# Local attention with the value product one step later, exponentials ahead of the transposed copy, and the row maxima of the cross stage sent from GpSimd's queue

## The chip, the cores and the metric

The kernel runs on one core of a Trainium2 chip. The core has five engines with a queue of instructions each: TensorE (PE in the profile; its weight loads are PEld), VectorE (DVE), ScalarE (ACT), GpSimd (POOL) and SyncE (SP, which here only starts transfers). The queues run side by side and meet only at semaphores. The metric is the device time of one call in microseconds (us), lower is better, taken as the median of three runs.

## What is computed

A batch of 16 rows of 256 tokens and 128 features goes first through one gated cross attention (16 heads of 8) over 1601 context tokens, then through six layers of local attention (16 heads of 64, window 32 and the window before it) and a gated feed-forward.

```python
x = x + jnp.tanh(g_xattn[0]) * xattn(layernorm(x), ctx, ctx, mask, ...)   # softmax over 1601 keys, 16 heads of 8
x = x + jnp.tanh(g_ffn[0]) * ffn(layernorm(x), ...)
# ffn: six times
    x = attn_layer(shift_tokens(x), Wqkv[i], q_scale[i], k_scale[i], Wo[i]) + x
    x = ffn_layer(shift_tokens(x), ln_g[i], ln_b[i], W1[i], b1[i], W2[i], b2[i]) + x
# attn_layer: q and k are brought to length 1, scaled and rotated; then, in each window of 32 queries,
    sim = jnp.einsum('bhwie,bhwje->bhwij', bq, bk2) * QK_SCALE     # keys of this window and the one before
    attn = jax.nn.softmax(jnp.where(mask, -max, sim), -1)
    out = jnp.einsum('bhwij,bhwje->bhwie', attn, bv2)              # then @ Wo
```

## The kernel before

The program has two stages, one behind the other. Nothing is scheduled by a compiler: each engine's queue is written out by hand, and every hand-over is a semaphore wait.

**Cross stage** (`cross_phase`, the first third of the span). It walks over the 16 rows. A row is four quarters `q` of four heads each, and a quarter is 13 key tiles `kt`. For each tile TensorE forms scores in `b_e` (mask L746, then product L750) in two halves, ScalarE exponentiates them to `eT` (L431), and TensorE multiplies them with the values (L652). Beside it the maxima of the next quarter are found (`b_s` L732, VectorE L506) and turned into 4 x 256 numbers `mneg`. `max_parts` (L348 on) splits these on GpSimd into three bf16 parts `mp` with five small operations; three transfers of 2 KB put the parts into rows of the operand `q_op`. Before, the transfers are issued by ScalarE, at tile 9 of each quarter (L475); TensorE waits for them (`mrow_in`) at tile 0 of the next quarter. In the first quarter of a row GpSimd also takes the rest of the key split, `kf` (L368), ahead of `max_parts`, and the last key part `kp` behind it (L384).

**Local stage** (`ffn_phase`, the other two thirds). It walks over 6 x 16 layer-rows. An iteration works on four rows at once, in different states: A makes q, k and v (`b_qk`, L1441 and L1452), B has its scores and probabilities made, C finishes them and goes through the output projection and the first feed-forward product, D ends with the second one (`b_nv`, L1472). It has eight steps `k`, and in each a unit `u` (two pairs of heads for half the queries) passes these stations: `scores(k)` on TensorE into `b_sc` (L1359, L1368); the row maximum and its scaling on VectorE (L1267, then `nb` L1276); four exponentials with sums on ScalarE to `probs` (L1143); reciprocal on VectorE (L1212) and normalising on GpSimd (L1067) a step later; `transposes(u)` on TensorE into `b_pt` (L1380), the copy to `probsT` on ScalarE (L1130) and `values(u)` on TensorE into `b_o` (L1400), all two steps later. VectorE takes `b_o` to `oT` (L1204) in the even steps. `b_sc`, `b_pt` and `b_o` exist once; `scores(k)` waits for `exp_ready`, the exponentials of step k-1. At the end of an iteration ScalarE has a Gelu (L1182), which needs one activation table load ahead of it and one behind it (L80).

"Step 7" and "unit 5" below are used in this sense; unit numbers run to 7 and belong to row B, or to row C where u = 8 + k - lag.

## Time and profile before

| | us |
|---|---|
| median of 3 runs (lowest, highest) | 5745.33 (5743.97, 5747.13) |
| profiled execution, its own time | 5749.15 |
| its span from first to last instruction | 5747.4 |
| TensorE busy in the span | 5416.8 (94%) |
| ScalarE, VectorE, GpSimd busy | 3999.1 (70%), 3635.8 (63%), 2655.9 (46%) |

Busy time of TensorE counts matmuls, whose ends are modelled. TensorE's granted clock is 0.992 of full speed as a mean over the span. A time in brackets behind a row of a timeline is how long that engine stood idle ahead of it, and after the arrow is what ended it. A wait or a time is that of the one profiled execution.

### The profile page before, as it was taken

To read this page: it belongs to the slowest core of one execution; us is meant where nothing else is said; L and a number is where in the kernel's file an instruction comes from. 1 tells how busy PE (TensorE), PEld (TensorE's weight loads), DVE (VectorE), ACT (ScalarE), POOL (GpSimd) and SP (SyncE) were. 2 spreads that over 40 slices of the span, in tenths; PEclk is the share of its full clock that TensorE was granted. 3 is DMA by queue.
4 is the path that set the end of the run, shared out by engine and by line. 5 is a ranking of instruction groups with operands and counts; after the bars stand their busy time and mean duration, and the time that the engine had idled before them with its cause. 6 is when DMAs were issued, how large, how long until landed. Compare 5 with 4: busy or idle time off the path is not lost.

```text
span 5747.4 us, 146588 instructions
## 1 busy us (share of the span) xinstructions
PE 5416.8 (94%) x51848; PEld 3320.3 (58%) x51848; DVE 3635.8 (63%) x8013; ACT 3999.1 (70%) x10790; POOL 2655.9 (46%) x2283
## 2 busy tenths in 40 slices
PE   6999999999999699999999999999999999999997
PEld 2444444444444366666666666666666666666665
DVE  5767766776677356665666666666666666656664
ACT  2555555555555378887788878787887778878885
POOL 2211221122111166566566656665666565666663
PEclk9999999999999899999999999999999999999999
DMA  3222232223322233333333333333333333333332
GB/s 86 67 74 65 66 76 74 65 62 79 76 65 56 74 100 102 94 108 105 98 97 97 120 93 97 97 113 100 97 101 105 105 97 98 99 111 104 94 97 89
DMA packets 144765, 517.20 MB, mean 90 GB/s; under 512 B 29872, under 2 KB 46128, under 8 KB 125616
## 3 DMA queue, kind: packets, MB, share of 16 engines
q1 hardware_dynamic: 142512, 507.43, 31.2%
q8 instruction: 427, 7.00, 0.5%
q14 instruction: 290, 2.38, 0.1%
q10 hardware_dynamic: 1536, 0.40, 0.0%
HBM read 224.98 MB, written 30.68 MB: 44 GB/s over the span
## 4 chain that ended last, share of the span: by engine, by line
PE 44%; ACT 12%; issue 6%; DVE 2%; POOL 1%; DMA 0%; SPq 0%; ACTq 0%; DVEq 0%; POOLq 0%
PE b_qk L1441 9%; PE b_c L1482 6%; PE b_pt L1380 5%; PE b_o L1400 5%; ACT probs L1143 5%; PE b_sc L1368 4%; PE b_nv L1416 3%; PE b_qk L1452 3%; PE b_sc L1359 2%; ACT L1182 2%; ACT L80 2%; PE b_c L1512 2%; PE b_nv L1512 1%; ACT ln_n L1108 1%; PE b_c L1487 1%
## 5 line engine op out<-in xcount | busy, mean ns | idle before, releaser
L431 ACT ACTIVATE eT<-b_e 128x512 f32<-128x512 f32 (+1 forms) x1664 | 903.3, 594 | 839.9 <-PE b_e L750 729.7
L1143 ACT ACTIVATE probs<-b_sc,nb,rq 128x96 f32<-128x96 f32 (+1 forms) x3072 | 1324.2, 449 | 9.2 <-DVE nb L1276 8.0
L506 DVE CUSTOM_DVE_ANT_0 junk<-b_s,mq 128x1024 bf16<-128x1024 f32 (+1 forms) x1024 | 995.2, 989 | 394.3 <-PE b_s L732 375.9
L1067 POOL TENSOR_TENSOR probs<-probs,rsums 128x512 f32<-128x512 f32 (+1 forms) x768 | 717.9, 935 | 673.1 <-DVE rsums L1212 672.4
L1267 DVE TENSOR_REDUCE b_sc<-b_sc 128x4 f32<-128x512 f32 (+1 forms) x768 | 486.2, 633 | 839.7 <-PE b_sc L1368 839.7
L1130 ACT ACTIVATE probsT<-b_pt 128x512 f32<-128x512 f32 x768 | 456.3, 594 | 583.0 <-PE b_pt L1380 583.0
L1441 PE MATMUL b_qk<-xs,weights 128*128 128x256 f32 x3072 | 740.7, 384 | 59.2 <-ACT sq L1157 31.2
L746 PE MATMUL b_e<-mk,identb 128*128 128x512 bf16 (+1 forms) x1664 | 638.4, 384 | 25.7 <-ACT eT L431 25.2
L1143 ACT ACTIVATION_READ_ACCUMULATOR probs<-b_sc,nb,rq 128x1 f32 x3072 | 645.4, 210 | 0.0
L1441 PEld LDWEIGHTS b_qk<-xs,weights 128*128 128x128 f32 x3072 | 556.6, 191 | 145.1 <-issue 74.5
L750 PE MATMUL b_e<-q_op,k_op 75*128 75x256 bf16 (+1 forms) x3328 | 639.3, 273 | 0.0
L1400 PEld LDWEIGHTS b_o<-probsT,v 128*64 128x64 f32 x9216 | 373.4, 137 | 453.2 <-issue 453.2
L1246 DVE TENSOR_TENSOR rot_s<-b_qk,rot_tab 128x512 f32<-128x512 f32 x768 | 525.4, 684 | 126.8 <-PE b_qk L1441 114.3
L1036 POOL TENSOR_TENSOR kT<-kT,rot_p 128x1024 f32<-128x1024 f32 x192 | 455.0, 2370 | 307.5 <-DMA rot_p<-rot_s 289.7
L732 PE MATMUL b_s<-k_op,q_op 72*128 72x512 bf16 (+1 forms) x2048 | 508.4, 342 | 44.9 <-DVE smax L506 36.3
L1400 PE MATMUL b_o<-probsT,v 128*64 128x64 f32 (+1 forms) x9216 | 516.0, 247 | 34.1 <-DVE oT L1204 26.7
L1157 ACT ACTIVATE sq<-b_qk 128x512 f32<-128x512 f32 x768 | 439.9, 599 | 123.9 <-DVE kT L1252 66.2
L1380 PE MATMUL b_pt<-ident,probs 128*128 128x128 f32 x3072 | 504.6, 287 | 1.7 <-POOL probs L1067 1.6
L1044 POOL TENSOR_TENSOR kT<-kT,rkb 128x1024 f32<-128x1024 f32 x192 | 452.5, 2357 | 104.3 <-DMA rkb<-rk_scr 104.3
L1036 POOL TENSOR_TENSOR qT<-qT,rot_p 128x1024 f32<-128x1024 f32 x192 | 453.3, 2361 | 91.2 <-DMA rot_p<-rot_s 78.5
L750 PEld LDWEIGHTS b_e<-q_op,k_op 75*128 75x128 bf16 (+1 forms) x3328 | 332.8, 100 | 245.6 <-issue 5.2
L652 PE MATMUL b_pv<-eT,vx 128*9 128x256 f32 x6656 | 442.8, 382 | 0.0
(133 smaller groups left out, 8406.7 us busy)
## 6 DMA issues: line engine op xcount, KB each, us to landing
rot_p<-rot_s SPq DMA_DIRECT2D x768, 256.0 KB, 2.4
rkb<-rk_scr SPq DMA_DIRECT2D x192, 512.0 KB, 6.4
k_op<-k_scr SPq DMA_DIRECT2D x192, 300.2 KB
v<-v SPq DMA_DIRECT2D x192, 256.0 KB, 3.6
k_scr<-kp SPq DMA_DIRECT2D x48, 400.2 KB, 3.5
weights<-in_ffn_w SPq DMA_DIRECT2D x27, 512.0 KB, 4.8
ctxT<-in_ctx SPq DMA_DIRECT2D x17, 800.5 KB, 8.6
q_op<-q_scr SPq DMA_DIRECT2D x144, 64.0 KB
```

Source lines behind the costliest of these rows:

```text
L431: nc.scalar.activation(eT[0:n, g % 4, i * 512:(i + 1) * 512], b_e[i][0:n, :], ACT.Exp).then_inc(s["e_ready"], 1)
L506: nc.vector.tensor_tensor_reduce(junk[:, half, 0:n], b_s[u % 2][:, 0:n], mq[:, p, qt, half * 1024:half * 1024 + n], 1.0, LOWEST, ALU.add, ...
L732: last = nc.tensor.matmul(b_s[u % 2][:, c * 512:c * 512 + n], q_op[0:MROW, p, 4 * sq + h, qt * P:(qt + 1) * P], k_op[sq][0:MROW, h, k0:k0 ...
L746: nc.tensor.matmul(b_e[i][0:n, :], identb[0:n, 0:n], mk[0:n, p, kt, :].unsqueeze(1).to_broadcast([n, 2, S]), start=True, stop=False, skip_ ...
L750: last = nc.tensor.matmul(b_e[i][0:n, j * S:(j + 1) * S], k_op[q][0:MROW + 3, 2 * i + j, kt * P:kt * P + n], q_op[0:MROW + 3, p, 4 * q + 2 ...
L1036: nc.gpsimd.tensor_tensor(dst, dst, rot_p[:, i % 2, :].rearrange("p (j t) -> p j t", j=4), ALU.add).then_inc(s["sum_ready"], 1)
L1067: nc.gpsimd.tensor_tensor(pu, pu, rsums[:, u % 2, :].unsqueeze(2).to_broadcast([P, 4, w]), ALU.mult).then_inc(s["pn_ready"], 1)
L1143: last = nc.scalar.activation(probs[:, t, k % 2, 2 * e + h, c0:P], b_sc[:, 512 * e + h * w:512 * e + (h + 1) * w], ACT.Exp, bias=nb[:, k % ...
L1246: nc.vector.tensor_tensor(per_block(rot_s[:, q % 2, 512 * (i % 2):512 * (i % 2 + 1)]), per_block(src), rot_tab[:, tab + 1, :].unsqueeze(1) ...
L1380: last = nc.tensor.transpose(b_pt[:, i * P:(i + 1) * P], probs[:, t, u % 2, i, :], ident[:, :])
L1400: last = nc.tensor.matmul(b_o[r, o0 + q0:o0 + q1], v[:, p, tile, vc], probsT[:, u % 2, c + q0:c + q1], start=True, stop=True, skip_group_c ...
L1441: last = nc.tensor.matmul(b_qk[:, 512 * (i % 2) + x * S:512 * (i % 2) + (x + 1) * S], weights[:, c0:c0 + P], xs[:, p, :], start=True, stop ...
```

## The change

It has two parts that don't touch each other.

In the local stage `values` runs with lag 3 in place of 2 and stands in TensorE's queue between `scores` and `transposes`, where it stood behind the projections. On ScalarE the four exponentials of a step stand ahead of the copy to `probsT`. For this `probs` has four buffers for each half in place of two, and the exponentials wait for the reciprocal two units back (`rsum_ready`) and for the transposes of the row before.

In the cross stage the three transfers of `mp` leave ScalarE's queue at tile 9 and go to GpSimd's queue, behind the five operations of the split and ahead of the last key part (first quarter) or of the mask `mk` (second quarter). The semaphore `mrow_in` is no longer among those started ahead by SyncE.

```diff
@@ cross_phase, gpsimd: iteration
                     if row:
                         max_parts(row, q)
+                        b, p = row
+                        sq, m = (q + 1) % 4, max_index(q)
+                        pool.wait_ge(s["mp_ready"], count("mp_ready", b, m))
+
+                        pool.wait_ge(s["e_done"], count("e_done", b, 8 * KT, back=2))
+                        for c in range(3):
+                            pool.dma_start(q_op[MROW + c:MROW + c + 1, p, 4 * sq:4 * sq + 4, :], mp[:, c, :]
+                                           ).then_inc(mrow_in, 16)
@@ cross_phase, scalar: iteration
-                        if kt == 9:
-
-                            item = (cur, q + 1) if q < 3 else (nxt, 0)
-                            if item[0]:
...
-                                act.wait_ge(s["mp_ready"], count("mp_ready", bm, m))
-
-                                act.wait_ge(s["e_done"], count("e_done", bm, 8 * KT, back=2))
-                                for c in range(3):
-                                    act.dma_start(q_op[MROW + c:MROW + c + 1, p, 4 * sq:4 * sq + 4, :], mp[:, c, :]
-                                                  ).then_inc(s["mrow_in"], 16)
@@ cross_phase, tensor: tile 0 of a quarter
-                                pe.wait_ge(s["mrow_in"], count("mrow_in", b, 48 * (q + 1)))
+                                pe.wait_ge(mrow_in, b * MROWS + 48 * (q + 1))
@@ ffn_phase
-        probs = sb("probs", [P, 2, 2, 4, P])
+        probs = sb("probs", [P, 2, 4, 4, P])
@@ ffn_phase, scalar: step k
-                    row, u = unit_at(B, C, k, 2)
-                    if row:
-                        n = row[0]
-                        act.wait_ge(s["pt_done"], count("pt_done", n, u + 1))
-
-                        act.wait_ge(s["o_done"], count("o_done", n, u - 1))
-                        nc.scalar.activation(probsT[:, u % 2, :], b_pt[:, :], ACT.Copy).then_inc(s["pt_kept"], 1)
...
-                        act.wait_ge(s["pt_done"], count("pt_done", n, k - 1))
+                        act.wait_ge(s["pt_done"], count("pt_done", n, k + 1, back=1))
+                        act.wait_ge(s["rsum_ready"], count("rsum_ready", n, k - 1))
...
                         last.then_inc(s["exp_ready"], 1)
+                    row, u = unit_at(B, C, k, 2)
+                    if row:
+                        n = row[0]
+                        act.wait_ge(s["pt_done"], count("pt_done", n, u + 1))
+
+                        act.wait_ge(s["o_done"], count("o_done", n, u - 1))
+                        nc.scalar.activation(probsT[:, u % 2, :], b_pt[:, :], ACT.Copy).then_inc(s["pt_kept"], 1)
@@ ffn_phase, tensor: step k
                     if B:
                         scores(k)
+                    row, u = unit_at(B, C, k, 3)
+                    if row:
+                        values(row, u)
                     row, u = unit_at(B, C, k, 2)
                     if row:
                         transposes(row, u)
...
-                    if row:
-                        values(row, u)
```

TensorE's queue in the local stage, step 0 of an iteration and what stands ahead of it: `b_sc` is the scores, `b_pt` the transposes, `b_o` the values, `b_qk` the projections, `b_nv<-hT` the second feed-forward product. Line numbers of the changed kernel differ by up to three here. Before:

```order
L1359 MATMUL b_sc<-lmask,identb 64x256 [waits exp_ready,kn_ready,sum_ready]
L1359 MATMUL b_sc<-lmask,identb 64x256 x3
L1368 MATMUL b_sc<-kT,qT 64x128 x8
L1380 MATMUL b_pt<-ident,probs 128x128 [waits pt_kept,pn_ready]
L1380 MATMUL b_pt<-ident,probs 128x128 x3
L1441 MATMUL b_qk<-xs,weights 128x256 [waits v_kept,part_in1,xs_ready]
L1441 MATMUL b_qk<-xs,weights 128x256
L1441 MATMUL b_qk<-xs,weights 128x256 [waits v3_kept]
L1441 MATMUL b_qk<-xs,weights 128x256
L1400 MATMUL b_o<-probsT,v 64x64 [waits o_kept,vmid_in,pt_kept,v3_kept,v_kept]
L1400 MATMUL b_o<-probsT,v 64x64 x7
L1472 MATMUL b_nv<-hT,weights 128x256 [waits hh_ready,part_in5]
```

Now:

```order
L1357 MATMUL b_sc<-lmask,identb 64x256 [waits exp_ready,kn_ready,sum_ready]
L1357 MATMUL b_sc<-lmask,identb 64x256 x3
L1366 MATMUL b_sc<-kT,qT 64x128 x8
L1398 MATMUL b_o<-probsT,v 64x64 [waits o_kept,vmid_in,pt_kept,v3_kept,v_kept]
L1398 MATMUL b_o<-probsT,v 64x64 x7
L1378 MATMUL b_pt<-ident,probs 128x128 [waits pt_kept,pn_ready]
L1378 MATMUL b_pt<-ident,probs 128x128 x3
L1442 MATMUL b_qk<-xs,weights 128x256 [waits v_kept,part_in1,xs_ready]
L1442 MATMUL b_qk<-xs,weights 128x256
L1442 MATMUL b_qk<-xs,weights 128x256 [waits v3_kept]
L1442 MATMUL b_qk<-xs,weights 128x256
L1471 MATMUL b_nv<-hT,weights 128x256 [waits hh_ready,part_in5]
```

The values moved from behind the projections to right behind the scores; what stood around them kept its order.

ScalarE's queue from step 7 to step 0 of the next iteration: `probs` is the exponentials, `probsT` the copy, `gg` the Gelu, the two table loads stand at its sides. Before:

```order
L1130 ACTIVATE probsT<-b_pt 128x512 [waits o_done,pt_done]
L1143 ACTIVATE probs,psums<-b_sc,nb,rq 128x96 [waits pt_done,nb_ready]
L1143 ACTIVATE probs,psums<-b_sc,nb,rq 128x96 x3
L1182 ACT_TABLE_LOAD [waits hh_ready]
L1182 ACTIVATE gg<-gt 128x768 [waits h_kept]
L1130 ACTIVATE probsT<-b_pt 128x512 [waits o_done,pt_done]
L80 ACT_TABLE_LOAD
L1143 ACTIVATE probs,psums<-b_sc,nb,rq 128x128 [waits pt_done,nb_ready]
L1143 ACTIVATE probs,psums<-b_sc,nb,rq 128x128 x3
L1157 ACTIVATE sq<-b_qk 128x512 [waits norm_done,rotc_ready] x2
```

Now:

```order
L1134 ACTIVATE probs,psums<-b_sc,nb,rq 128x96 [waits rsum_ready,pt_done,nb_ready]
L1134 ACTIVATE probs,psums<-b_sc,nb,rq 128x96 x3
L1145 ACTIVATE probsT<-b_pt 128x512 [waits o_done,pt_done]
L1180 ACT_TABLE_LOAD [waits hh_ready]
L1180 ACTIVATE gg<-gt 128x768 [waits h_kept]
L80 ACT_TABLE_LOAD
L1134 ACTIVATE probs,psums<-b_sc,nb,rq 128x128 [waits rsum_ready,pt_done,nb_ready]
L1134 ACTIVATE probs,psums<-b_sc,nb,rq 128x128 x3
L1145 ACTIVATE probsT<-b_pt 128x512 [waits o_done,pt_done]
L1155 ACTIVATE sq<-b_qk 128x512 [waits norm_done,rotc_ready] x2
```

The copy of step 7 now stands behind that step's exponentials, ahead of the table load for the Gelu; that of step 0 stands behind the exponentials of step 0, ahead of the two squares.

GpSimd's queue in the cross stage, first quarter of a row: `kf` and `kp` are parts of the keys, `mp` the split maxima, `mq` a mask. Before:

```order
L358 TENSOR_TENSOR mres<-mres,mp 4x256 [waits mmid_ready]
L361 CAST mp<-mres 4x256 [waits mres2_ready]
L384 TENSOR_TENSOR kp<-kf,kp 128x1601 [waits kmid_ready]
L390 TENSOR_SCALAR mq<-m 128x3202 [waits m8_in,s_max]
L373 TENSOR_TENSOR qf<-qf,qp 128x256 [waits qhi_ready]
L376 TENSOR_TENSOR qp<-qf,qp 128x256 [waits qmid_ready]
```

Now:

```order
L360 TENSOR_TENSOR mres<-mres,mp 4x256 [waits mmid_ready]
L363 CAST mp<-mres 4x256 [waits mres2_ready]
L389 DMA q_op<-mp 1x4x256 [waits e_done,mp_ready]
L389 DMA q_op<-mp 1x4x256 x2
L394 TENSOR_TENSOR kp<-kf,kp 128x1601 [waits kmid_ready]
L400 TENSOR_SCALAR mq<-m 128x3202 [waits m8_in,s_max]
L375 TENSOR_TENSOR qf<-qf,qp 128x256 [waits qhi_ready]
L378 TENSOR_TENSOR qp<-qf,qp 128x256 [waits qmid_ready]
```

Three transfers stand behind the last operation of the split, where there were none.

## Rows read from the trace of the kernel before

**Rows 1.** One iteration: us; busy PE, PEld, DVE, ACT, POOL; clock; DMA share; GB/s
```profile
4207.40:4245.89 38.49, 37.24 (x387) 25.19 (x388) 23.91 (x58) 30.97 (x94) 23.48 (x19) 1.00 0.32 98
```

**Rows 2.** Waits of TensorE, 2100 to 5740 us: total us, times, longest us
```profile
PE b_sc L1359 <- ACT probs L1143: 58.9, 90, 0.7
PE b_qk L1441 <- ACT sq L1157: 27.0, 92, 0.3
PE b_o L1400 <- DVE oT L1204: 26.4, 96, 1.2
PE b_o L1400 <- ACT probsT L1130: 7.2, 7, 2.1
```

**Rows 3.** Timeline of TensorE, steps 6 to 1: start us, length us, idle before
```profile
4231.49 0.28 PE L1359 MATMUL b_sc<-lmask,identb 64*64 64x192 bf16 x4
...
4233.79 0.69 PE L1400 MATMUL b_o<-probsT,v 128*64 128x64 f32 x16 [0.25 <-DVE oT L1204]
...
4236.33 0.28 PE L1359 MATMUL b_sc<-lmask,identb 64*64 64x192 bf16 x4
...
4240.06 0.30 PE L1359 MATMUL b_sc<-lmask,identb 64*64 64x256 bf16 x4
...
4240.73 0.66 PE L1380 MATMUL b_pt<-ident,probs 128*128 128x128 f32 x4
...
4243.05 0.69 PE L1400 MATMUL b_o<-probsT,v 128*64 128x64 f32 x16
4243.70 1.53 PE L1472 MATMUL b_nv<-hT,weights 128*128 128x256 f32 x6
4245.89 0.30 PE L1359 MATMUL b_sc<-lmask,identb 64*64 64x256 bf16 x4 [0.66 <-ACT probs L1143]
```

**Rows 4.** Timeline of ScalarE, steps 7 to 0
```profile
4237.56 0.60 ACT L1130 ACTIVATE probsT<-b_pt 128x512 f32<-128x512 f32 x1 [2.10 <-PE b_pt L1380]
4238.05 0.43 ACT L1143 ACTIVATE probs<-b_sc,nb,rq 128x96 f32<-128x96 f32 x1
...
4241.12 0.84 ACT L1182 ACTIVATE gg<-gt 128x768 f32<-128x768 f32 x1
4241.87 0.58 ACT L1130 ACTIVATE probsT<-b_pt 128x512 f32<-128x512 f32 x1
...
4245.43 0.21 ACT L1143 ACTIVATION_READ_ACCUMULATOR probs<-b_sc,nb,rq 128x1 f32 x1
4245.52 1.09 ACT L1157 ACTIVATE sq<-b_qk 128x512 f32<-128x512 f32 x2
```

**Rows 5.** Timeline of VectorE, steps 6 to 0
```profile
4232.84 0.69 DVE L1204 COPY oT<-b_o 128x512 f32<-128x512 f32 x1
4233.45 0.48 DVE L1301 SCALAR_TENSOR_TENSOR xg<-b_c,par,rstd 128x256 f32<-128x256 f32 x1
...
4237.61 0.16 DVE L1276 TENSOR_TENSOR nb<-b_sc,rq 128x4 f32<-128x4 f32 x1
...
4242.29 0.47 DVE L1228 SCALAR_TENSOR_TENSOR hT<-b_nv,bias,gg 128x256 f32<-128x256 f32 x1
```

**Rows 6.** Waits of TensorE in the cross stage, 200 to 1900 us
```profile
PE b_e L746 <- ACT eT L431: 18.4, 28, 1.0
```

**Rows 7.** Timeline of GpSimd, one split of the first quarter
```profile
926.42 0.39 POOL L361 CAST mp<-mres 4x256 bf16<-4x256 f32 x1 [0.17 <-POOL mres L358]
```

**Rows 8.** Timeline of ScalarE, the sends behind that split
```profile
926.84 1.80 ACTq L475 DMA_DIRECT2D q_op<-mp  x3
928.74 1.08 ACT L431 ACTIVATE eT<-b_e 128x512 f32<-128x512 f32 x2 [3.46 <-issue]
```

**Rows 9.** Timeline of TensorE behind those sends, to the second quarter
```profile
929.39 0.39 PE L746 MATMUL b_e<-mk,identb 128*128 128x512 bf16 x1 [0.94 <-ACT eT L431]
...
931.79 0.41 PE L746 MATMUL b_e<-mk,identb 65*65 65x512 bf16 x1 [0.43 <-ACT eT L431]
...
934.61 0.38 PE L746 MATMUL b_e<-mk,identb 128*128 128x512 bf16 x1
```

More of the change, by code:

```diff
@@ L167, in cross_phase @@
         dma_per = dict(xa_in=16, xb_in=16, x1_kept=16, xn_kept=16, ctx_in=16, m8_in=16, mt8_in=16, kscr_in=48,
-                       qscr_in=48, qop_in=9 * 16, mrow_in=4 * 48)
+                       qscr_in=48, qop_in=9 * 16)
         s = {n: sem(n) for n in (*per, *dma_per)}
@@ L172, in cross_phase @@
         KOP = 3 * 16
+        mrow_in, MROWS = sem("mrow_in"), 4 * 48
         pool_passed = sem("pool_passed_x")
@@ L350, in max_parts @@
                 pool.wait_ge(s["mneg_ready"], count("mneg_ready", b, m))
-                wait_apart(pool, pool_passed, s["mrow_in"], count("mrow_in", b, 48 * (m - 1)))
+                if b or m > 1:
+                    wait_apart(pool, pool_passed, mrow_in, b * MROWS + 48 * (m - 1))
                 nc.gpsimd.tensor_copy(mp[:, 0, :], mneg[:, :]).then_inc(s["mhi_ready"], 1)
@@ L1065, in iteration @@
                         pool.wait_ge(s["rsum_ready"], count("rsum_ready", n, u + 1))
-                        pu = probs[:, t, u % 2, :, c0:P]
+                        pu = probs[:, t, u % 4, :, c0:P]
                         nc.gpsimd.tensor_tensor(pu, pu, rsums[:, u % 2, :].unsqueeze(2).to_broadcast([P, 4, w]),
@@ L1143, in iteration @@
                                 last = nc.scalar.activation(
-                                    probs[:, t, k % 2, 2 * e + h, c0:P], b_sc[:, 512 * e + h * w:512 * e + (h + 1) * w],
+                                    probs[:, t, k % 4, 2 * e + h, c0:P], b_sc[:, 512 * e + h * w:512 * e + (h + 1) * w],
                                     ACT.Exp, bias=nb[:, k % 2, e, h:h + 1], scale=rq[:, p, t, j0 + h, e:e + 1],
@@ L1379, in transposes @@
                     for i in range(4):
-                        last = nc.tensor.transpose(b_pt[:, i * P:(i + 1) * P], probs[:, t, u % 2, i, :], ident[:, :])
+                        last = nc.tensor.transpose(b_pt[:, i * P:(i + 1) * P], probs[:, t, u % 4, i, :], ident[:, :])
                     last.then_inc(s["pt_done"], 1)
```

3 lines of the change are left out of this document (removed).

## The prediction

> **What bounds the kernel now.** I began with the two stages as windows. In the local stage one iteration takes 38.49 us, and TensorE is busy for 37.24 of them at a granted clock of 1.00, ScalarE for 30.97, VectorE for 23.91 and GpSimd for 23.48 [rows 1]. So TensorE is the bound, and no change of order can bring back more than its idle time. That is read from its waits. Over the local stage they are few and each has one place: 90 before the scores of step 1 (58.9 us), 92 before the projections of step 3 (27.0 us), 96 before the values of step 6 (26.4 us), all but the first kind a quarter of a microsecond, and 7 at the end of the program, where no row A gives TensorE other work (7.2 us) [rows 2]. Together 119.5 us, 2.1% of 5745: the ceiling for this part. The timeline of one iteration shows where each wait comes from [rows 3 to 5]. In the cross stage TensorE waits 28 times, 18.4 us in all, for ScalarE's exponentials [rows 6]; I looked up what ScalarE did just before [rows 8].
>
> **The local stage, wait by wait.**
>
> *Scores of step 1 (0.66 us).* They wait for the exponentials of step 0 [rows 3]. Back from there ScalarE is without a pause to step 7: copy, exponentials, table load, Gelu, copy, table load, exponentials [rows 4]. What starts that run is the only thing that counts. Scores of step 7 start at 4236.33, VectorE's `nb` ends at 4237.61 + 0.16 = 4237.77, but the exponentials start at 4238.05, since the copy stands ahead of them (4237.56, its follower 0.49 later) [rows 3 to 5]. With the copy behind them they wait only for `nb`. How long ScalarE needs from VectorE's signal no row shows: from ScalarE's last accumulator read (4245.43 + 0.21 = 4245.64) to the scores at 4245.89 it is 0.25 on TensorE [rows 3, 4], and at the least 0. I take 0.05, since a ScalarE that stands ready goes on within less than a tenth where its rows follow each other. The start is 4237.82, 0.23 earlier; the ends are 0.03 and 0.28. The copies cancel: the one of step 7 now lies between exponentials and Gelu (+0.49), the one of step 0 leaves the place between Gelu and table load (4241.87 to the end at 4242.45, less the overlap with the Gelu, again 0.49). So 0.66 becomes 0.43, and 90 times 0.23 are **21 us**.
>
> *Values of step 6 (0.25 us).* They wait for VectorE's `oT` copy, which ends at 4232.84 + 0.69 = 4233.53; they start at 4233.79 [rows 3, 5]. With lag 3 the `oT` copy they need was made a step earlier: this wait is gone. What is late next is the product behind them, which needs `xg`: it ends at 4233.45 + 0.48 = 4233.93, and with the same 0.26 to TensorE may start at 4234.19. TensorE without its wait would be there at 4233.54 + 0.65 (the length of the values, 4243.05 to 4243.70 [rows 3]) = 4234.19. A tie; I keep 0.03 back. 96 times 0.22 are **21 us**.
>
> *Projections of step 3 (0.29 us).* They wait for ScalarE's squares behind the norms' logarithm and exponential. Between the norms and these projections TensorE still has scores, values and transposes, in another order, and ScalarE still starts with the norms: unchanged.
>
> *End and beginning.* Without row A the values wait for the fresh copy, 7.2 us in 7 waits [rows 2]; with lag 3 the copy is a step old. The step is then bound by the exponentials instead. I take **5 us** of 0 to 10.
>
> *What costs nothing, and its cover.* Values now need the copy of the step before soon after the scores. Worst case is step 1: the copy starts where the squares did, 4245.52, takes 0.60, and may be seen 0.25 later, 4246.37; scores (0.67, from 4240.06 to 4240.73) started at 4245.89 end at 4246.56. 0.19 us are left; past them each 0.1 us costs 0.1 in each of 96 iterations. The squares of step 0 stand behind the copy and end their first half near 4246.7; TensorE asks for it only after scores, values and transposes, near 4247.7. The Gelu ends 0.49 - 0.23 = 0.26 later, at 4242.22, and VectorE starts on its product at 4242.29 as before [rows 4, 5]; here only 0.07 is left. `probs` has buffers enough, its waits are for work a row old. The one extra semaphore per step I count as nothing; 0.05 each on the run from step 7 to step 1 would cost 0.1 x 90 = 9 us.
>
> *The order on TensorE itself.* The same matmuls run, but the values now stand between scores (64 x 64 tiles) and transposes. No row shows these two neighbours. Where the values have other neighbours, and nothing is late, they start with no idle time ahead [rows 3], so I take 0; the other end is a quarter microsecond, a release that isn't hidden, which in 8 x 96 = 768 steps would be 192 us.
>
> **The cross stage.** In the first quarter of a row the split ends late, at 926.42 + 0.39 = 926.81 [rows 7], because GpSimd has a long key operation ahead of it. ScalarE stands at its transfers until then, issues three in 1.80 us, and goes on at 928.74, after 3.46 us [rows 8]. TensorE waits 0.94 and 0.43 us for it [rows 9]. Both waits go when the transfers go. 28 waits are 14 rows of two; the last row of 16 has no key work, so 15 rows: 18.4 x 15/14 = 19.7 us. VectorE's maxima are close behind at this place; I take **18 us**.
>
> GpSimd then issues the transfers, with the last key part queued behind them, which I cost at nothing: SyncE comes to the stores of the keys only behind the row's other stores, in the second quarter. What can be late is the rows themselves: TensorE asks for them at 934.61 [rows 9], with the gain at 933.3, so 6.5 us after the split. How long GpSimd needs for one transfer no row shows. Below it is ScalarE's 0.60, so 1.8 for three; above I take three times that, 5.4, which leaves 1.1 us to land and would give a wait of 1 to 2 us in 15 rows, some 25 us. I take the lower half: no wait. The other quarters have the same split and several microseconds more.
>
> ScalarE's transfers cost 0.60 us each to issue [rows 8]. The Trainium skill (DMA: Bandwidth & Descriptors, section on the anatomy of one DMA) puts a GpSimd transfer at some 2.0 us fixed, whatever its size; an estimate of three issues at 1 us and 2.0 us to land would be 5.0 us, 1.5 inside the limit, and by it the sum stays as it is.
>
> **The sum.** 21 + 21 + 5 + 18 = 65 us. The profiled execution took 5749.15 (span 5747.4), 3.8 above the median of the runs, so 5684 for it and 5745.33 - 65 = **5680 us** for the median: 1.1% faster.
>
> **Rivals.**
>
> *1. The wait before step 1 stays (chance 0.12).* If the run on ScalarE has a slack that I don't see, or the extra semaphores eat the 0.23, only 21 + 5 + 18 are won: 5701. For it: 0.23 is the difference of two close ends. Against: ScalarE shows no pause in the run.
>
> *2. The rows come late (0.12).* GpSimd's transfers take over 6.5 us in the first quarter. At 9 us the wait is 2.5 us in 15 rows: 65 - 37 = 28 us are won, 5717; it would need 10.8 us to undo the whole change. VectorE's instructions here are 0.5 to 0.7 us [rows 5]; if each of three issues had to let one of them pass, that adds 2.1 us to 1.8 and still leaves 2.6 to land. The Trainium skill (SBUF — State Buffer, section "SBUF: two separate sides", on the "DVE blocks DMA" trap) says that a GpSimd transfer's descriptors can't be written while VectorE works in a two-port mode; that is this rival's mechanism, and no run here shows it yet.
>
> *3. Slower: values between scores and transposes (0.08).* One mechanism: a gap at the new neighbours in each of 768 steps. It decides from 65/768 = 0.085 us a step; at 0.12 it is 92 us, 5772. For it: no row shows the pair. Against: none of the pairs that are shown has a gap.
>
> *4. More than forecast (0.08).* The waits of step 1 and step 3 go as well, with all of the end: up to 119.5 + 20, 5610.
>
> **How the numbers follow.** Forecast 0.60, and by the bounds above (0.03 to 0.28 in step 1, 0 to 10 at the ends, 9 for semaphores, up to 25 for late rows) its own range is 5655 to 5708. To hold 8 in 10 it reaches over rivals 1 and 2 to 5718 and a little into 4, 5640. About 0.2% (11.5 us) is what a measurement of this kernel can tell from no change. Faster: forecast, 1, 4 and most of 2, 0.86; same 0.06, slower 0.08.
>
> **What would show it.** Right: one iteration takes about 38.05 us; `b_sc` waits 0.43 in step 1; no wait of `b_o` for `oT`; 0.29 before `b_qk` stays; in the cross stage no wait of `b_e` for `eT` and none at tile 0. Wrong: waits of `b_o` for `probsT` in step 1, of `b_nv` for `hT`, of the first `b_e` of a second quarter for a transfer, or iterations longer with no wait named.

## The result, and the profile after

The changed kernel takes **5611.65 us** (median of 4 runs, 5604.57 to 5615.04), beside 5746.23 us for the kernel before on the same chip: ratio 0.9763, 95% interval 0.9746 to 0.978. That is 2.4% faster, 134.6 us, twice the 65 that were forecast, and outside the range. The profiled span fell by 137.7 us, from 5747.4 to 5609.7. The first scores of the local stage start at 1967.98 in place of 2001.06, so 33.1 us of that lie in the cross stage (forecast 18) and 104.6 in the local stage (forecast 47).

One iteration of the local stage, a window from the scores of a step 1 to the next (columns as in [rows 1]):

```profile
4185.86:4223.14 37.28, 36.40 (x388) 25.36 (x388) 24.02 (x57) 30.98 (x94) 23.52 (x19) 1.00 0.34 101
```

It is 1.21 us shorter than the window in [rows 1]. ScalarE, VectorE and GpSimd do the same work in it, and the clock is 1.00 in both. But TensorE, with the same matmuls (387 records before, 388 now; some can be missing from a trace), is busy for 36.40 us in place of 37.24. No wait explains that; it is the first thing to see. The waits of TensorE, 2100 to 5600 us of the changed kernel (total us, times, longest us):

```profile
PE b_sc L1357 <- ACT probs L1134: 37.3, 90, 2.1
PE b_qk L1442 <- ACT sq L1155: 26.7, 91, 0.3
PE b_nv L1471 <- DVE hT L1226: 18.2, 60, 2.2
```

Against [rows 2], the wait of `b_sc` shrank, the one of `b_qk` stayed, both of `b_o` are gone, and `b_nv` has a new one for `hT`. The few single waits of up to 2.2 us are at the borders of layers and in the last iterations, where the gain is smaller: the usual iteration went from 38.50 to 37.28 (median of 95 distances between equal steps), the mean from 38.65 to 37.54. The timeline of TensorE from step 6 to step 1 is the counterpart of [rows 3]:

```profile
4213.82 0.28 PE L1357 MATMUL b_sc<-lmask,identb 64*64 64x192 bf16 x4
...
4214.35 0.69 PE L1398 MATMUL b_o<-probsT,v 128*64 128x64 f32 x16
4214.97 0.66 PE L1378 MATMUL b_pt<-ident,probs 128*128 128x128 f32 x4
...
4217.35 0.30 PE L1357 MATMUL b_sc<-lmask,identb 64*64 64x256 bf16 x4
...
4221.20 1.53 PE L1471 MATMUL b_nv<-hT,weights 128*128 128x256 f32 x6 [0.18 <-DVE hT L1226]
4223.14 0.30 PE L1357 MATMUL b_sc<-lmask,identb 64*64 64x256 bf16 x4 [0.40 <-ACT probs L1134]
```

ScalarE in the same place (counterpart of [rows 4]) and VectorE (of [rows 5]):

```profile
4215.30 0.43 ACT L1134 ACTIVATE probs<-b_sc,nb,rq 128x96 f32<-128x96 f32 x1 [1.75 <-DVE nb L1274]
```

```profile
4215.10 0.16 DVE L1274 TENSOR_TENSOR nb<-b_sc,rq 128x4 f32<-128x4 f32 x1
...
4219.79 0.48 DVE L1226 SCALAR_TENSOR_TENSOR hT<-b_nv,bias,gg 128x256 f32<-128x256 f32 x1
```

`nb` ends at 4215.10 + 0.16 = 4215.26 and the exponentials start 0.04 later. `hT` starts 4219.79 - 4213.82 = 5.97 behind the scores of step 7, against 5.96 before. TensorE's product with `hT` could start at 4221.20 - 0.18 = 4221.02, 7.20 behind those scores, against 7.37 before [rows 3]: `hT` is not later, TensorE is earlier.

In the table, each step runs from its scores to the next scores, and the listed waits inside it are taken off (us; one iteration of each kernel, from the timeline of TensorE):

| step | 0 | 1 | 2 | 3 | 4 | 5 | 6 | 7 | TensorE's own time | waits |
|---|---|---|---|---|---|---|---|---|---|---|
| before | 5.17 | 5.52 | 4.57 | 5.74 | 4.21 | 3.76 | 4.59 | 3.73 | 37.29 | 1.20 |
| after | 5.20 | 5.33 | 4.59 | 5.54 | 4.22 | 3.51 | 4.48 | 3.53 | 36.40 | 0.87 to 0.91 |

About 0.3 us of the gain are waits, and 0.9 us are TensorE's own time, 0.2 in each of the steps 1, 3, 5, 7 and 0.1 in step 6. (Where a group runs into a wait, the table counts its whole modelled length, 1.89 us for the projections of step 0, in place of the 1.73 or 1.82 after which the next group starts. So a gain in the steps 0 and 6 is partly hidden.) What the shortened steps have in common is seen in the weight loads. Step 1 before, the matmuls:

```profile
4246.56 0.66 PE L1380 MATMUL b_pt<-ident,probs 128*128 128x128 f32 x4
4247.05 1.89 PE L1441 MATMUL b_qk<-xs,weights 128*128 128x256 f32 x8
4248.87 0.69 PE L1400 MATMUL b_o<-probsT,v 128*64 128x64 f32 x16
4249.49 1.99 PE L1482 MATMUL b_c<-oT,weights 128*128 128x256 f32 x8
4251.41 0.30 PE L1359 MATMUL b_sc<-lmask,identb 64*64 64x256 bf16 x4
```

The weight loads of the same two groups before:

```profile
4248.87 0.55 PEld L1400 LDWEIGHTS b_o<-probsT,v 128*64 128x64 f32 x16 [0.33 <-issue]
4249.49 1.59 PEld L1482 LDWEIGHTS b_c<-oT,weights 128*128 128x128 f32 x8
```

And in step 1 of the changed kernel, matmuls, then the weight load of the output projection:

```profile
4187.64 1.89 PE L1442 MATMUL b_qk<-xs,weights 128*128 128x256 f32 x8
4189.37 1.89 PE L1481 MATMUL b_c<-oT,weights 128*128 128x256 f32 x8
4191.19 0.30 PE L1357 MATMUL b_sc<-lmask,identb 64*64 64x256 bf16 x4
```

```profile
4189.15 1.70 PEld L1481 LDWEIGHTS b_c<-oT,weights 128*128 128x128 f32 x8
```

Behind the values (tile 128*64) the output projection's load starts together with its matmuls, at 4249.49, and the group lasts until 4251.41, 1.92 us. Behind another 128*128 group the load starts 0.22 us ahead of the matmuls and the group takes 1.82 us. The projections of `b_qk` ahead of the values take 4248.87 - 4247.05 = 1.82, ahead of a group of their own width 4189.37 - 4187.64 = 1.73. So the theory to test: TensorE pays for a change of tile between two groups, about 0.1 us on either side of it. (The experiments speak of tile width, since 128 and 64 columns are what differs here.) The scores (64*64) and the values (128*64) used to stand apart, with four changes of tile in most steps; side by side they leave three, and one change less is 0.2 us. In the steps 2 and 4, where the values stood beside a 128*32 group, the number stays the same, four and five, and so do the lengths in the table.

In the cross stage, GpSimd's sends and what follows them, in the first quarter of a row of the changed kernel:

```profile
909.74 1.56 POOL L389 DMA_DIRECT2D q_op<-mp  x3 [0.30 <-POOL mp L363]
911.31 3.04 POOL L394 TENSOR_TENSOR kp<-kf,kp 128x1601 bf16<-128x1601 f32 x1
```

Three transfers are issued in 1.56 us (0.52 each, ScalarE needed 0.60), and TensorE's waits for `eT` between 200 and 1900 us are down from [rows 6] to this, with none at tile 0 of the next quarter:

```profile
PE b_e L743 <- ACT eT L441: 2.0, 8, 0.3
```

### The profile page after: what moved, and what is told of

It reads as the page before. It is cut to its first block, busy times and chain, and to the rows that moved or that the text cites. A ratio compares the mean times of both kernels' runs of the same rounds, so it can differ in the third digit from the quotient of the medians.

```text
span 5609.7 us, 146586 instructions
## 1 busy us (share of the span) xinstructions
PE 5327.1 (95%) x51848; PEld 3343.6 (60%) x51848; DVE 3637.7 (65%) x8013; ACT 4000.9 (71%) x10790; POOL 2759.8 (49%) x2475
## 4 chain that ended last, share of the span: by engine, by line
PE 43%; ACT 13%; issue 4%; DVE 2%; DMA 1%; POOL 1%; SPq 0%; ACTq 0%; DVEq 0%; POOLq 0%
PE b_qk L1442 9%; PE b_c L1481 6%; ACT probs L1134 5%; PE b_o L1398 5%; PE b_pt L1378 5%; PE b_qk L1453 4%; PE b_sc L1366 4%; PE b_nv L1414 3%; PE b_sc L1357 2%; ACT L1180 2%; ACT L80 2%; PE b_c L1511 2%; PE b_nv L1511 1%; ACT gg L1180 1%; ACT ln_n L1105 1%
## 5 line engine op out<-in xcount | busy, mean ns | idle before, releaser
L1134 ACT ACTIVATION_READ_ACCUMULATOR probs<-b_sc,nb,rq 128x1 f32 x3072 | 619.4, 202 | 0.0
```

Of the source, the lines that this page charges most:

```text
L1134: last = nc.scalar.activation(probs[:, t, k % 4, 2 * e + h, c0:P], b_sc[:, 512 * e + h * w:512 * e + (h + 1) * w], ACT.Exp, bias=nb[:, k % ...
```

## The experiments

In all of them "before" ran on the same chip, at 5747.5 to 5750.9 us. Intervals are those of the ratio to it.

### The two halves alone

One kernel has the cross stage of after and the local stage of before, the other the reverse; no other edit.

> The kernel before with only the cross part of the change (transfers of the split maxima from GpSimd). The first scores of the local stage start at 2001.06 us in the trace before and at 1967.98 in the changed kernel: theory A, the two parts are independent and the cross part is worth those 33 us, so 5713 us. Rival B, as in the prediction, only the named waits of b_e for eT are worth anything (18 us): 5728, and the rest of the 33 comes from the start of the local part.

> The kernel before with only the local part. If the parts are independent (A): 135 less 33 = 102 us won, 5644 us, and 37.28 us for an iteration. If they help each other (B), the two single gains don't add up to 135.

Measured: the cross stage alone 5718.94 us (0.9932 to 0.9965), 28.5 less than before; the local stage alone 5638.61 us (0.9793 to 0.9826), 108.9 less. The gains add up to 137.4, beside 134.6 for both together, so the halves hardly act on one another: theory A of the second run. The first stands between theory A's 5713 and rival B's 5728, nearer to A; its local stage starts at 1970.96, 30.1 us earlier than before. Both halves brought more than forecast.

### Values put later, in three ways

First the changed kernel with the values of three steps ago behind the projections, as the values stood before:

```diff
+                    row, u = unit_at(B, C, k, 3)
+                    if row:
+                        values(row, u)
                     if D and k == 0:
```

(and the same three lines taken from their place behind the scores). Then the kernel before, with its values of two steps ago moved behind the projections of `b_c`, to the end of the step.

> The changed kernel, lag 3 and exponentials first kept, but the values stand again behind the projections, ahead of the group that follows them. Theory A (neighbours): 0.9 us of the 1.22 us that an iteration won are weight loads that can be pulled ahead again once the 64-column tiles of the values no longer stand between two groups with 128-column tiles. Then this kernel gives it back: iteration about 38.2 us, time about 5700. Rival B (waits): the 1.22 us are waits of which the trace names only a part; those are as in the changed kernel, so 5612 and 37.3 us.

> The kernel before in all else (lag 2, copy first, two buffers of probs, transfers from ScalarE), but the values stand last in each step, next to the scores of the following step. Theory A (neighbours): one change of tile width less in the six steps that have other work, so 0.9 us of an iteration, and the 0.25 us wait for oT goes too; the wait of 0.66 before the scores of step 1 stays: iteration about 37.35 us, time about 5640. Rival B (lag 3 or exponentials first are what helps): no gain but the 0.25, iteration 38.25, time 5722.

Measured: 6345.99 us (1.1024 to 1.1061), far slower than either theory said, and 5802.53 us (1.008 to 1.0113), slower by 0.97%. Neither is a clean test of neighbours, since both brought new waits. In the first, one of VectorE's waits, 2050 to 5600 us:

```profile
DVE oT L1202 <- PE b_o L1398: 667.4, 314, 3.0
```

VectorE copies `oT` ahead of its other work in a step, and now stands there until the values of the same step are through. With three steps' distance the values have to come early in the step for that copy's sake. With TensorE's own waits, 7.1 us, taken off, the usual iteration is back at 37.4 us, the own time of before; with so many waits that is a rough number. In the second, the work behind the old place of the values is asked for 0.6 us earlier and meets `hT`, `xs`, `xg` and `gt` not ready. The largest of TensorE's waits, with `xs` and `xg` close behind at 50.1 and 48.2 us:

```profile
PE b_nv L1470 <- DVE hT L1228: 50.7, 87, 0.6
```

But with the waits taken off (39.10 less 2.49), its iteration is 36.61 us of TensorE's own time, against 37.29 before: 0.7 us less by an order alone, the exponentials and the distance of two steps unchanged.

### One part of the new order undone at a time

The copy put ahead of the exponentials again on ScalarE; the transposes put ahead of the values on TensorE, distance kept; and ScalarE's new order with the values two steps behind at their old place. The second is this edit and nothing else:

```diff
                         scores(k)
-                    row, u = unit_at(B, C, k, 3)
-                    if row:
-                        values(row, u)
                     row, u = unit_at(B, C, k, 2)
                     if row:
                         transposes(row, u)
+                    row, u = unit_at(B, C, k, 3)
+                    if row:
+                        values(row, u)
```

> The changed kernel with one thing put back: on ScalarE the copy of the transposed probabilities stands ahead of the exponentials again; TensorE keeps the new order (values of three steps ago right behind the scores). Theory A (most of the unforeseen gain is TensorE's own time, because the matmuls of the values, 128x64 tiles, no longer stand between two groups of 128x128 tiles): the steps 0, 1, 3, 5 and 7 stay as short as in the changed kernel, b_qk's group at 1.73 and the output projection's at 1.82, and only the scores of the first step wait longer for the exponentials, 0.66 in place of 0.40: 37.5 us an iteration, 96 times 0.25 more, 5636 us. Rival B (the gain comes with the exponentials going first): the local stage falls back to most of its old length, over 5690 us.

> The changed kernel with TensorE's values (of three steps ago) put behind the transposes in place of ahead of them: scores, transposes, values, projections. Nothing else moves, and no engine has to deliver earlier than before, but the queue has one change between 128x64 and 128x128 tiles more in each of the eight steps. Theory A (each such change costs TensorE about 0.1 us and more, a place between two 128x128 groups about 0.2): 0.8 to 1.6 us an iteration, 5690 to 5760 us, with the projections of b_qk back at the long duration. Rival B (the gain comes from when probabilities and values are ready, not from the neighbours): 5605 to 5620 us, the iteration at 37.3 us.

> The changed kernel with one part undone on TensorE: the values are again those of two steps ago and stand behind the projections, as in the kernel before; ScalarE keeps its new order, exponentials ahead of the copy. The values then need a copy that ScalarE makes in the same step only after its exponentials (some 1.9 us behind the start of them). Theory A (the longer distance of three steps is what lets the exponentials go first): TensorE waits for the copy in most steps, 0.3 to 1.5 us each, and the local stage is far longer than before, over 5850 us. Rival B (the copy is ready in time at this place too, and three steps are not needed): 5660 to 5740 us, with the wait of the first step's scores at 0.4 us.

*Transposes first:* 5739.55 us (0.9976 to 0.9995), inside theory A's 5690 to 5760. That is 9 us less than before, and the cross stage alone gives 28.5: the local stage is now longer than before. The waits fell (0.73 us an iteration in place of 1.20), yet the iteration is 38.74 in place of 38.50. Own time is 38.00, 1.6 us above the changed kernel's 36.40: one change of tile more in each of eight steps, 0.2 each. Its timeline in step 1:

```profile
4184.08 0.66 PE L1378 MATMUL b_pt<-ident,probs 128*128 128x128 f32 x4
4184.66 0.69 PE L1398 MATMUL b_o<-probsT,v 128*64 128x64 f32 x16
4185.28 2.00 PE L1442 MATMUL b_qk<-xs,weights 128*128 128x256 f32 x8
4187.11 1.89 PE L1481 MATMUL b_c<-oT,weights 128*128 128x256 f32 x8
```

The transposes take 4184.66 - 4184.08 = 0.58 us ahead of the values, and before 4247.05 - 4246.56 = 0.49 ahead of a group of their own width. Behind the values, the group of `b_qk` takes 4187.11 - 4185.28 = 1.83 in place of 1.73. So more than TensorE's new order had gained was undone by three lines that add no wait.

*Copy first:* 5792.13 us (1.0061 to 1.0094), slower than before and far over A's 5636; by the number it is rival B (over 5690), and more than B said, since the local stage is longer than its old length. By the mechanism it is neither: TensorE's own time is 36.48 us, short as A says, and the waits are 2.8 us. ScalarE shows why, in step 7:

```profile
4207.99 0.60 ACT L1127 ACTIVATE probsT<-b_pt 128x512 f32<-128x512 f32 x1 [1.76 <-PE b_pt L1378]
4208.49 0.42 ACT L1141 ACTIVATE probs<-b_sc,nb,rq 128x96 f32<-128x96 f32 x1
```

The transposes now stand behind the values, the copy waits for them, and exponentials queued behind the copy wait too: TensorE waits 268 times for them, 222.1 us between 2050 and 5600. A was wrong that only 0.25 us an iteration would come back.

*Exponentials first with two steps' distance:* 6603.06 us in one run, over 5850 as A said. The waits of TensorE, 2050 to 5600 us:

```profile
PE b_o L1398 <- ACT probsT L1145: 687.6, 593, 1.8
```

The values wait for a copy that now comes behind the exponentials. The three parts of the local edit (exponentials first, distance three, values beside the scores) belong together: with any one of them left out, the iteration is longer than the 38.50 us of before (39.24, 48.19 and 38.74 us). In the first two that comes from new waits, in the third from TensorE's own time.

### Is it the tile width? Two pairs of twins

The first pair adds, in steps 0 to 3 between transposes and projections, two useless matmuls with 64 columns, with 128*64 tiles in one and 128*128 in the other:

```diff
+                            if i == 2 * k:
+                                cz = (W_QK + INNER if i < 4 else W_QK) + 2 * (i % 4) * P
+                                for z in range(2):
+                                    nc.tensor.matmul(b_qk[z * DH:(z + 1) * DH, 0:DH], weights[:, cz:cz + DH],
+                                                     xs[:, p, 0:DH], start=True, stop=True, skip_group_check=True)
```

> The changed kernel with work added that nothing uses: in the steps 0 to 3, between the transposes and the projections of b_qk, two more matmuls of 128x64 tiles with 64 columns (their output is overwritten by the projections right behind them). It is to be read against its twin, with two matmuls of 128x128 tiles and as many columns in the same place. By the trace of the changed kernel eight such narrow matmuls of the values take 0.62 us, so two of them 0.16 us. Theory A (a change of tile width between neighbours costs TensorE some 0.1 us on either side): 0.16 + 0.2 us in each of four steps, 1.4 us an iteration less what waits take in (at most 0.4): 5700 to 5750 us, and longer than the twin by 0.3 to 0.8 us an iteration, 30 to 75 us. Rival B (only the work counts, and narrow tiles load fewer weights): 0.16 us a step, at most 0.65 us an iteration, 5640 to 5675 us, and no longer than the twin.

> The changed kernel with work added that nothing uses: in the steps 0 to 3, between the transposes and the projections of b_qk, two more matmuls of 128x128 tiles with 64 columns, whose neighbours on both sides are 128x128 tiles as well. By the trace of the changed kernel a transpose of a 128x128 tile with 128 columns takes 0.12 us, so these two between 0.16 and 0.25 us. Theory A and rival B agree here: 0.6 to 1.0 us an iteration less what waits take in, 5640 to 5700 us. They differ in where the twin with narrow tiles stands: above it by 30 to 75 us (A), or at most level with it (B).

Measured: 5726.79 us (0.994 to 0.997) with narrow, 5747.74 us (0.9984 to 1.0003) with wide tiles. The order of the totals is B's; the narrow total is in A's 5700 to 5750, and the wide one over the 5700 that both theories had as its upper end. The rows of the narrow kernel, step 0, and then of the wide one:

```profile
4207.53 0.66 PE L1378 MATMUL b_pt<-ident,probs 128*128 128x128 f32 x4
4208.12 0.34 PE L1443 MATMUL b_qk<-xs,weights 128*64 128x64 f32 x4
4208.39 1.99 PE L1447 MATMUL b_qk<-xs,weights 128*128 128x256 f32 x8
```

```profile
4187.84 0.66 PE L1378 MATMUL b_pt<-ident,probs 128*128 128x128 f32 x4
4188.34 0.56 PE L1443 MATMUL b_qk<-xs,weights 128*128 128x64 f32 x4
4188.73 1.95 PE L1447 MATMUL b_qk<-xs,weights 128*128 128x256 f32 x8
```

With narrow tiles behind them the transposes take 0.59 in place of 0.49, as A has it, and `b_qk` has the longer 1.99 (in the changed kernel 1.89). With wide tiles behind them they take 0.50: what lengthens them is not that something stands there, but its tile. But the wide filler itself takes 0.39 us start to start, where I had priced 0.16 to 0.25, against 0.27 for the narrow one. The pair differs in two things at once, so its total decides nothing. The second pair mends that: in every step the same two narrow matmuls, once ahead of the four transposes (beside the values), once between the second and the third (`i == 2`):

```diff
                     for i in range(4):
+                        if i == 0:
+                            for z in range(2):
+                                nc.tensor.matmul(b_pt[z * DH:(z + 1) * DH, i * P:i * P + DH], ident[:, 0:DH],
+                                                 probs[:, t, u % 4, 0, 0:DH], start=True, stop=True,
+                                                 skip_group_check=True)
```

> The changed kernel with the same useless work in every step as its twin: two matmuls of 128x64 tiles with 64 columns, here right behind the values (128x64 tiles too) and ahead of the four transposes. Their output is overwritten by the transposes. No change of tile width is added. By the earlier pair of runs two such matmuls take 0.16 to 0.27 us, so 1.2 to 2.1 us an iteration, less what waits take in: 5700 to 5810 us. Theory A (TensorE pays about 0.2 us for narrow matmuls between wide ones, by their place and not by their work) and rival B (the work alone counts) agree here and differ in the twin.

> The changed kernel with the same two useless matmuls of 128x64 tiles in every step, now between the second and the third of the four transposes (128x128 tiles): the same instructions, the same waits, the same buffers and banks as in the twin, three instructions later in TensorE's queue. Theory A (a change of tile width costs about 0.1 us on either side): 0.2 us a step, 1.6 us an iteration above the twin, 120 to 170 us longer than the twin. Rival B (the work alone counts): within 20 us of the twin.

Measured: 5643.56 us (0.9799 to 0.9831) beside the values, 5771.62 us (1.0025 to 1.0053) between the transposes. **128 us lie between two kernels with the same instructions, waits and buffers**, inside A's 120 to 170 and far from B's 20. The first:

```profile
4206.61 0.69 PE L1403 MATMUL b_o<-probsT,v 128*64 128x64 f32 x16
4207.12 0.29 PE L1380 MATMUL b_pt<-probs,ident 128*64 128x64 f32 x4
4207.34 0.66 PE L1383 MATMUL b_pt<-ident,probs 128*128 128x128 f32 x4
4207.83 1.89 PE L1447 MATMUL b_qk<-xs,weights 128*128 128x256 f32 x8
```

and the second:

```profile
4206.20 0.69 PE L1403 MATMUL b_o<-probsT,v 128*64 128x64 f32 x16
4206.82 0.44 PE L1383 MATMUL b_pt<-ident,probs 128*128 128x128 f32 x2
4207.19 0.34 PE L1380 MATMUL b_pt<-probs,ident 128*64 128x64 f32 x4
4207.45 0.44 PE L1383 MATMUL b_pt<-ident,probs 128*128 128x128 f32 x2
4207.73 1.89 PE L1447 MATMUL b_qk<-xs,weights 128*128 128x256 f32 x8
```

From values to projections it is 4207.83 - 4206.61 = 1.22 us in the one and 4207.73 - 4206.20 = 1.53 in the other. Beside the values the two matmuls add only 0.11 to the 1.11 of the changed kernel. Own times are 37.10 and 39.09 us, 0.25 a step apart; of these 2.0 us an iteration 0.6 are taken from waits that the longer kernel no longer has. The first kernel was cheaper than the 5700 I had put as its lower end, since I had priced the two matmuls with their changes.

The twins differ in one more thing: in the second one TensorE also goes more often between plain matmuls and transposes (`nc.tensor.transpose`). That this is not the price is seen where no transposes take part: in the kernel before, step 1, the output projection takes 1.92 us behind the values, and behind a plain group of its own tile 1.82; and the transposes ahead of the wide filler, plain matmuls too, keep 0.50.

Nor is it the width alone. In the kernel with the values at the end of each step they stand ahead of the scores, both 64 wide (128*64 and 64*64):

```profile
4202.87 0.69 PE L1400 MATMUL b_o<-probsT,v 128*64 128x64 f32 x16
4203.49 0.30 PE L1359 MATMUL b_sc<-lmask,identb 64*64 64x256 bf16 x4
```

The values take 4203.49 - 4202.87 = 0.62 us there, as ahead of 128*128 groups (0.61 to 0.62), and 4207.12 - 4206.61 = 0.51 ahead of another 128*64 group in the first kernel above. So a change between two narrow shapes costs too, and what counts is the shape of the tile, rows and columns. This was read from rows; no run was made for it.

### What the cross stage gained

The kernel before, with ScalarE's sends one key tile later in the first quarter only:

```diff
-                        if kt == 9:
+                        if kt == (10 if q == 0 else 9):
```

> The kernel before with one edit in the cross stage: ScalarE issues the three transfers of the split maxima one key tile later (at tile 10 in place of 9) in the first quarter of each row; everything else as before. In the kernel before ScalarE first waits some 1.5 us for GpSimd's split and then issues for 1.8 us. Theory A (two costs add up, and each is part of the 33 us that the cross stage gained): the wait for the split goes, the issue stays, the wait of TensorE for eT shrinks to about half: 8 to 18 us less than before, 5730 to 5740 us. Rival B (the issue of 1.8 us alone decides, the wait for the split is slack): 5742 to 5748 us, no change. Rival C (the wait for the split alone decides): 5715 to 5722 us, as with GpSimd sending.

Measured: 5715.72 us (0.9926 to 0.9959), 33 us less, all that moving the sends to GpSimd had won (28.5 us alone). Rival C, which I had given the least room. ScalarE there, in the same place of a row:

```profile
910.03 1.54 ACT L450 ACTIVATE kp<-kf 128x1601 bf16<-128x1601 f32 x1
910.13 1.80 ACTq L475 DMA_DIRECT2D q_op<-mp  x3
912.24 1.08 ACT L431 ACTIVATE eT<-b_e 128x512 f32<-128x512 f32 x2 [0.67 <-PE b_e L750]
```

The 1.80 us of issuing go on while ScalarE's cast of 1.54 still runs, and the exponentials behind wait for TensorE, not for the issue. So the price was ScalarE standing in front of a split that wasn't ready; at this later place the issue itself lay in slack. Whether it would at tile 9, no run shows.

### Taking out the waits that were left

On top of the changed kernel: the copy of step 7 on VectorE, and then also the first square of step 2 ahead of the norms' Ln and Exp. The second edit is this:

```diff
-                    if A and k == 2:
-                        inverse_norms(0, rn_k)
                     if A and k < 4:
                         n = A[0]
                         for i in (2 * k, 2 * k + 1):
+                            if i == 5:
+                                inverse_norms(0, rn_k)
```

> The changed kernel with one edit: in step 7 of an iteration the copy of the transposed probabilities to SBUF is done by VectorE, ahead of the copy of v, in place of by ScalarE, whose run of exponentials, copy, table load, Gelu, table load, exponentials there ends late in two of the three waits of TensorE that are left. Theory A (these waits, 0.40 for the exponentials and 0.20 for hT, are ScalarE's run and nothing else): both shrink by up to 0.49 us of copy, the iteration by 0.4 to 0.6 us, 5555 to 5575 us. Rival B (VectorE, which has the gate's copies and hT in the same place, becomes late by the same amount): the wait for hT grows instead and the time stays between 5600 and 5625 us.

> The changed kernel with the copy of step 7 on VectorE, as before, and one more edit on ScalarE: in step 2 the square of the first projection goes ahead of the Ln and Exp of the norms in place of behind them. TensorE waits 0.29 us for that square in step 3 of each iteration (27.3 us in all), and Ln and Exp take 1.35 us of ScalarE ahead of it. Theory A (that wait is nothing but Ln and Exp ahead of the square): the wait goes, nothing else grows, 0.29 us an iteration, 5546 us (5540 to 5555). Rival B (the keys' scales or the second group of norms come late by the 0.6 us that Ln and Exp now wait): a new wait for ln or kn as long as the old, 5565 to 5585 us.

Measured: 5573.61 us (0.9678 to 0.9711), in A's range, and **5539.17 us** (0.9618 to 0.9644), a little under A's 5540 to 5555; rival B is excluded in both. The second is the fastest kernel of this study, 3.7% faster than before, some 72 us below the changed kernel. Its regular waits have gone but for one of 0.17 us before the scores of step 1; the largest between 2050 and 5600 us are:

```profile
PE b_c L1491 <- POOL xs L1073: 11.9, 22, 1.8
PE b_sc L1362 <- issue: 10.9, 63, 0.2
```

Half of what is left of TensorE's idle time are single waits of over 0.9 us at the borders of layers and in the last iterations. The usual iteration is 36.43 us with 36.3 of TensorE's own time, so a much faster kernel from here needs fewer or cheaper matmuls, or fewer changes of tile.

## Why the prediction was wrong, by its own steps

**The step that failed is "The order on TensorE itself".** It said that no row shows the new neighbours, took 0, and gave as the other end a loss. It never asked what the *old* neighbours cost. One change of tile in six of the eight steps, which the new order does away with, cost 0.9 us an iteration: with 96 iterations some 85 us at the most, more than the whole forecast. The rows were in the trace of before: the output projection's group is 1.92 us behind the values, `b_qk`'s 1.82 ahead of them. I looked for listed idle time between groups ("none of the pairs that are shown has a gap"), but this cost is inside the groups' spacing and counts as busy. For the same reason the sentence that no change of order can bring back more than idle time was false. The Trainium skill (TensorEngine Tiling (Array Packing), section "Key Properties" under "Tiling Modes") says it outright: "Changing tiling mode (not just tile) drains the TensorE". It gives no price; the trace agrees, with 0.2 us for one change more in *transposes first* and 0.25 to 0.31 us for the two more of the twins. By its words a change between 64*64 and 128*64 counts as well; the rows with the values ahead of the scores bear that out in that one direction. I hadn't weighed that page.

*Scores of step 1.* Right: 0.66 to 0.40, forecast 0.43; the exponentials start 0.04 behind `nb`, estimated 0.05. That the wait itself agrees is luck in part: TensorE came through step 7 in 0.20 us less, which would have made it longer, and the new wait for `hT` took in 0.18 of that. From the scores of step 7 to those of step 1 it is 9.56 us before and 9.32 after, 0.24 less, just what the exponentials start earlier.

*Values of step 6.* Right that the wait for `oT` goes. But a wait for `hT` came in step 0, 0.18 to 0.22 us, which I had listed as a sign of error. The cover that I put at 0.07 us held as far as VectorE goes (5.97 against 5.96); TensorE arrives 0.17 us earlier, because step 7 is itself 0.20 shorter. So waits gave about 0.3 us an iteration where 0.45 was forecast.

*Projections of step 3.* Right: 0.29 stayed. The last experiment took it away by moving one square.

*End and beginning.* The 5 us didn't come. The waits of the values at the end fell from 7.2 to 0.4 us, but from the last full iteration's first scores to the end of the span it is 74.8 us before and 75.1 after.

*Cross stage.* Right in mechanism and mis-sized: 33.1 us in place of 18. The row (start of one operation of GpSimd to the same one in the next row) went from 115.36 to 113.33 us, 2.03 less in most of the 16. I had summed the two waits in [rows 9] alone, 1.37. Matched matmul by matmul, the two kernels part by 1.51 us at these waits and by 0.53 more early in the second quarter. There VectorE's `xq`, which the next matmuls need, took 0.97 us before and takes 0.41 after:

```profile
936.60 0.97 DVE L612 TENSOR_TENSOR xq<-lc,lrs 128x256 f32<-128x256 f32 x1
```

```profile
917.70 0.41 DVE L609 TENSOR_TENSOR xq<-lc,lrs 128x256 f32<-128x256 f32 x1
```

Before, it fell into GpSimd's `mq` (934.44 to 937.31), which had been held up behind ScalarE's cast of `kp`; after, `mq` is over at 917.31. It is 0.97 in 13 of 16 rows of the kernel before and of the one with the local stage alone, and about 0.41 in at least 14 of 16 rows of the changed kernel, the cross stage alone and the sends at tile 10. No run was made for this alone. That GpSimd's sends cost nothing was right: no wait of TensorE for them appears. The rule of the Trainium skill that speaks against it (SBUF — State Buffer, section "SBUF: two separate sides", the "DVE blocks DMA" trap) shows no wait here.

*Rivals and range.* The third had the right place and the wrong sign. The fourth had nearly the right time, 5610 (5606 by its own sum), by a wrong mechanism: it took all waits to go, and 0.87 us of 1.20 stayed. The lower end of the forecast's own range, 5655, doesn't follow from the bounds that it names: they reach 4.5 + 5 us under 5680, to 5671.

## What to carry to other kernels

Before pricing a new order on TensorE, write down the tile shape of each group in the queue and count the changes, in the old order and in the new. Groups of one shape belong side by side; a group of another shape costs two changes inside a run of one shape, and only one more at a border that is there already. "Busy" is no floor: compare the start-to-start time of the same group behind different neighbours. When an engine sends a transfer that waits for another engine, first try to send it later; where it stands may cost more than who issues it, and an engine that stands there also holds up what others do next.

## What the runs showed of the hardware that was not expected

- A change of tile shape costs TensorE about 0.1 us on either side (0.49 to 0.58 for the transposes ahead of it, 1.73 to 1.83 for the projections behind it). It shows in no idle time, and the next weight load starts with its matmul in place of up to 0.22 us ahead. Between two narrow shapes the group ahead pays as much (values 0.62 ahead of 64*64, 0.51 ahead of 128*64).
- Two 128*128 matmuls with 64 columns took 0.39 us, two 128*64 ones 0.22 behind a group of their own shape and 0.27 between wide ones: with so few columns the wider tile was the dearer here.
- GpSimd issued a transfer in 0.52 us, ScalarE in 0.60, and ScalarE's issue ran beside its own activation.
- A 128x256 fp32 operation of VectorE took 0.97 us beside a long operation of GpSimd and 0.41 without it.
